# Three extra products of ones ahead of the second score pass, in seven of sixteen attention units

## What is computed

```python
x = x + tanh(g_xattn[0]) * L0_xattn(layernorm(x), ctx)   # 16 heads of 16, softmax over 256 keys
x = x + tanh(g_ffn[0])   * L0_ffn(layernorm(x))          # 8 routed experts (top 4, in groups) + 1 shared
x = x + tanh(g_xattn[1]) * L1_xattn(layernorm(x), ctx)   # scores clipped at +-10000
x = x + tanh(g_ffn[1])   * L1_ffn(layernorm(x))          # 8 experts of width 1024, top 2
```

## Time and profile before

| | |
|---|---|
| runs | 1160.27, 1165.95, 1166.85 us; median 1165.95 |
| profiled execution | 1160.78 us, of which the span from first to last instruction is 1159.0 |
| mean granted TensorE clock | 0.872 of full speed |
| PE busy | 957.9 us, 83% of the span |
| DVE busy | 768.1 us, 66% |
| ACT, POOL busy | 480.2 and 240.7 us |

### The profile page before, as it was taken

The page is one execution under the profiler, slowest core; times in us unless marked ns, Lnnn a source line. Parts: engine busy times, 40 slices in busy tenths (PEclk is TensorE's granted clock), DMA queues, the critical chain, the costliest instruction groups (busy, mean ns, idle before and its releaser), DMA issues.

```text
span 1159.0 us, 17921 instructions
## 1 busy us (share of the span) xinstructions
PE 957.9 (83%) x6385; PEld 758.5 (65%) x6385; DVE 768.1 (66%) x1607; ACT 480.2 (41%) x834; POOL 240.7 (21%) x389
## 2 busy tenths in 40 slices
PE   3578799999999899888897688782599799797993
PEld 2345577776767666656675455451599799797993
DVE  2544467757676677777777787754598588586681
ACT  1124444443434333323333333430367476475561
POOL 2011111010110010101000031110424344544443
PEclk9956899999999999899898665765599899899897
DMA  3985555054154161716267553230557665666552
GB/s 109 242 190 120 100 96 90 33 87 77 46 80 75 37 118 59 138 46 137 78 130 140 135 112 112 89 92 29 201 189 241 185 187 183 173 203 210 160 142 27
DMA packets 122055, 141.89 MB, mean 122 GB/s; under 512 B 11536, under 2 KB 106408, under 8 KB 121968
## 3 DMA queue, kind: packets, MB, share of 16 engines
q1 hardware_dynamic: 113136, 128.50, 44.7%
q0 software_dynamic: 8832, 12.25, 5.6%
HBM read 109.97 MB, written 30.75 MB: 121 GB/s over the span
## 4 chain that ended last, share of the span: by engine, by line
PE 36%; DVE 20%; issue 17%; DMA 11%; POOL 8%; ACT 5%; SPq 1%; POOLq 0%; DVEq 0%; ACTq 0%
DMA out_x<-x,token_i 8%; PE bank L752 6%; POOL out_x L1720 5%; DVE rowmax L1222 5%; PE value_bank L696 4%; PE bank L762 3%; DVE clipped L1247 3%; PE bank L723 3%; PE bank L607 3%; PE by_query L660 2%; PE bank L616 2%; PE by_key L681 2%; PE bank L646 2%; POOL xs_in L1707 2%; DVE x L1371 2%
## 5 line engine op out<-in xcount | busy, mean ns | idle before, releaser
L1222 DVE TENSOR_REDUCE rowmax<-by_query 128x4 f32<-128x1024 f32 x128 | 155.8, 1217 | 36.7 <-PE by_query L660 36.7
L1037 ACT ACTIVATE probs<-clipped 128x1024 f32<-128x1024 f32 x64 | 67.6, 1057 | 196.6 <-DVE clipped L1247 196.5
L1666 POOL TENSOR_SCALAR rstd<-moments 128x2 f32<-128x2 f32 x32 | 7.1, 223 | 591.4 <-DVE moments L1186 591.4
L1720 POOL DMA_INDIRECT out_x<-x,token_i x46 | 92.5, 2012 | 171.3 <-DMA out_x<-x,token_i 148.2
L912 PE MATMUL bank<-w_hi,h_hi 128*128 128x256 f32 x368 | 104.1, 283 | 0.0
L912 PE MATMUL bank<-w_lo,h_hi 128*128 128x256 f32 x368 | 104.1, 283 | 0.0
L912 PE MATMUL bank<-w_hi,h_lo 128*128 128x256 f32 x368 | 104.1, 283 | 0.0
L660 PE MATMUL by_query<-stack_k,stack_q 48*128 48x256 f32 x512 | 72.4, 365 | 33.8 <-DVE rowmax L1222 31.2
L660 PEld LDWEIGHTS by_query<-stack_k,stack_q 48*128 48x128 f32 x512 | 44.0, 212 | 76.1 <-DVE rowmax L1222 39.1
L681 PE MATMUL by_key<-stack_q,stack_k 50*128 50x256 f32 x512 | 69.6, 354 | 25.5 <-DVE clipped L1247 17.0
L696 PE MATMUL value_bank<-probs,values 128*32 128x256 f32 x1024 | 82.9, 450 | 7.8 <-ACT probs L1037 7.7
(11 more groups left out here) (237 smaller groups left out, 2252.4 us busy)
## 6 DMA issues: line engine op xcount, KB each, us to landing
w<-in_L_ffn_W SPq DMA_DIRECT2D x46, 1024.0 KB, 7.7
lower<-max SPq DMA_DIRECT2D x64, 256.0 KB, 3.4
stack_k<-qk SPq DMA_DIRECT2D x96, 128.0 KB, 5.0
stack_q<-qk SPq DMA_DIRECT2D x96, 128.0 KB, 7.4
qk<-hi SPq DMA_DIRECT2D x32, 256.0 KB, 4.1
qk<-lo SPq DMA_DIRECT2D x32, 256.0 KB, 4.6
rows<-w_gate SPq DMA_DIRECT2D x8, 264.0 KB, 3.9
x<-in_x SPq DMA_DIRECT2D x8, 256.0 KB, 6.7
```

The costliest lines, as they stand in the source:

```text
L1037: ac.activation(probs[i % 3][:, :, :, :].rearrange("p h k s -> p (h k s)"), src, ACT.Exp).then_inc(sem.exp_done, 1)
L1222: dv.tensor_reduce(rowmax[u % 2][:, 2 * p:2 * p + 2, :], by_query[:, :, :].rearrange("p h (t s) -> p h t s", t=TT), AX, ALU.max).then_inc( ...
L1720: po.indirect_dma_start(out[:, :], bass.IndirectOffsetOnAxis(ap=token_i[:, n:n + 1].bitcast(U32), axis=0), ysb[i % 3][:, t, :], None, comp ...
```

## The change

In units 0 to 2 and 12 to 15, behind the wait for the previous pass's reader and ahead of the four products of the second score pass, PE multiplies `ones_bf` by one column of `ones_bf` repeated 512 times, three times, into the first bank of `by_key`. The score products that follow start their sums anew, so they overwrite this. No other engine's work changes. That is 7 units x 8 passes x 3 = 168 products of 512 columns.

```diff
@@ -675,6 +675,9 @@
                 pe.wait_ge(sem.clip_done, i - PAIRS * NB)
             elif i:
                 pe.wait_ge(sem.exp_done, i)
+            if u < 3 or u >= UNITS - 4:
+                for _ in range(3):
+                    pe.matmul(by_key[:, 0, :], ones_bf[:, :], ones_bf[:, 0:1].broadcast_to([P, 512]), start=True, stop=True)
             for kt in range(2):
                 for side in range(2):
                     rows = slice(HALF * side, HALF * side + ROWS)
```

## The result

The changed kernel took 1170.79 us (median of six runs, 1169.78 to 1171.84) where the kernel before took 1166.4 in the same rounds (1160.27 to 1168.59): a ratio of 1.0057, 95% interval 1.0031 to 1.0082 (the quotient of the two medians alone is 1.0038, 4.4 us, inside that interval). It is slower by about 6.6 us, clear of noise and inside what the text had called no change. The profiled execution took 1170.28 us, its span 1168.5, mean clock 0.895 in place of 0.872.

A forecast was written before the change was run, and what follows sets the result against it. PE was taken to set the pace in units 3 to 11, with low-clock chain work in front and tail; +6.6 and -5.7 us gave +0.9 on 1160.8, 1161.7, plus 5.2 for the median: 1166, range 1147 to 1180.

The forecast's parts named there:

- within 1%: Whole kernel: a change under about 1% (11.7 us) counts as the same; chance 0.53, faster 0.26, slower 0.21.
- the front: Units 0 to 2: 4.4 us saved by the clock, 11.0 paid for ones on the chain, net +6.6 us.
- The tail: Units 12 to 15: 14.4 us saved by the clock, 7.7 paid on the chain, 1 elsewhere, net -5.7 us.
- the milder form of rival B: Tail: clock up but gain taken by DVE and DMA waits, 0 to +5 us; kernel 1173 to 1178; chance 0.14.
- the price bounds: 22 passes on the chain: 0.4 or 1.4 us per pass instead of the counted price, shifting the time -5 to +8.
- The price of the ones: Each pass with ones, on PE: three products cost 0.65 us at the high clock, 1.28 at the low one.
- The clock: Low stretches end after one or two slots: 82 to 137 us rises to about 0.85, units 12 to 15 to 0.8.
- Rival A: Front and tail: clock stays high from first ones to last, -17 us, so 1149; chance 0.26.
- B: Units 13 to 15, slot loop: low clock persists, tail +20 us, kernel 1193; 0.12 shared with ones not moving the clock.
- Unit 2: PE has 0.9 us idle in 42.3 at full clock, so nothing hides the ones: 0.65 us per chain pass.
- Units 0 and 1: First low stretch ends at about 98.6 us, not 105.4; 4.4 us saved, 6.4 paid, net +2.0.
- The other 24 passes are covered: Units 12 to 15: passes off the chain hide behind DVE's `rowmax` or finish stage and ACT, costing 1 us in all.

The follow-up runs named there:

- tail_thin: Against the kernel before: ones only in units 12 to 15, products cut to 32 rows and 32 columns, same 512 columns streamed; ratio 1.0156.
- mid_four: Against the kernel before: three products of ones per pass in units 3 to 6 only; ratio 1.0146.
- u01_only: Against the kernel before: three products of ones per pass in units 0 and 1 only; ratio 1.0014.
- front_only: Against the kernel before: three products of ones per pass in units 0 to 2 only; ratio 1.0073.
- front_thin: Against the kernel before: ones only in units 0 to 2, products cut to 32 rows and 32 columns, same 512 columns streamed; ratio 1.019.
- tail_only: Against the kernel before: three products of ones per pass in units 12 to 15 only; ratio 1.0019.
- tail_ahead: Against the kernel before: eight products of ones into the value bank, ahead of the wait, in passes 2 and 6 of units 12 to 15 only; ratio 1.0027.
- no2_x3: Against the kernel before: three products of ones per pass in units 0, 1 and 12 to 15, none in unit 2; ratio 1.0073.
- three doses: Against the kernel before: one, three or six products of ones per pass in units 12 to 15 only; ratios 0.9973, 1.0019, 1.0036.

## Why the prediction was right, and where not

The time, 1170.79, lies in the range, 4.8 us above the 1166 forecast, and "within 1%" was the likeliest case. The range was 33 us wide, though. Of the two halves of the sum the front came out about as forecast (+5.3 us for +6.6). The tail did not: there the milder form of rival B came true, given 0.14: the clock up, the gain taken. The 1173 to 1178 us given for it begin 2.2 us above the measured time, and the forecast lies 4.8 below it. So the number was right in part by luck. Two sums of the text are also off by themselves: 1161.7 + 5.2 is 1166.9, so its forecast was 1167, and the price bounds for 22 passes are 8.8 and 30.8 us against 18.7 counted, -10 and +12, not -5 and +8 (still inside the range). By its steps:

**The price of the ones.** Forecast 0.65 and 1.28 us a pass; at the high clock 0.65 was added to PE's row. At the low clock, 1.39 from the first ones to the scores with the start-up in it, as 0.74 is 0.65 with it. The rows of other products gave the right price, and the 131 ns a product that the Trainium skill has for a stream (page "TensorE: Matmul & The Clock Gate", section "Back-to-back issue gap") would have made it 0.39: the trace disagrees.

**The clock.** Forecast 0.85 in units 0 and 1 and 0.8 in units 12 to 15, measured 0.86 and 0.82. The stall ahead of the ones at about 126 us is still there (2.15 us, at 127.3), with the clock low behind it from 128.4 to 131.8; but the ones there ran before the fall, at the high clock, where 1.28 had been counted. Rival A (held high throughout) did not happen, nor B (stays low); tail_thin shows what B costs when it is made to happen, +18 us against the +20 that the rival gave for the tail. (The "64-row" score products of that part of the text have 48 and 50 rows in the trace.)

**Unit 2.** Forecast: nothing hides the ones. Seven of its passes stood on the chain, so the sum had 7 x 0.65 = 4.6, and 4.6 was measured. Place, sign and size were right, the size by two small errors that cancel: all eight passes pay, and some of the 0.9 us of idle time is filled. mid_four shows that filling idle time is the rule there. Unit 3 begins 5.0 us later (forecast: some 6), unit 12 6.0 later.

**Units 0 and 1.** Forecast 4.4 saved and the other 6.4 of the 11.0 paid, +2.0. Measured +0.7 us in the profiles of the changed kernel and of u01_only, -1.3 in that of front_only. The net is near; the terms look too small: front_thin shows that the ones without their clock cost these units 16.5 us (84.1 - 67.6), in part because the clock there was lower still than before.

**The tail: the step that failed.** "The other 24 passes are covered", "I count 1 in all", "Net -5.7 us." Measured +0.5 in the stretch and -0.7 from the last pass to the slot table (L869 at 817.67 before, its line at 823.46 after), -0.2 together, and tail_only excludes -5.7 for the kernel. The last pass begins 6 us later than 769.3, where the forecast said about 1. The chain of waits of the changed kernel in units 12 to 15 has ones in 16 places, not 8, and 9.1% of the 152.0 us from 624.6 us on, 13.8 us, not the 7.7 that I had counted:

```profile
by line: issue 9.2%; PE by_key L680 9.1%; DVE clipped L1250 8.8%; PE value_bank L699 7.9%; DMA w_down<-zalt_rows 7.7%; DVE rowmax L1225 6.0%; PE by_key L684 5.7%; PE bank L726 5.1%; PE bank L718 2.8%; PE bank L637 2.7%; PE by_query L660 2.6
```

I had taken the chain of before and asked which passes stood on it. With the ones in, passes came onto it that had not stood there: clip, ones, scores, clip again. That wait of DVE grew by 5.2 us (2.3 to 7.5) where I had counted 1, the largest single piece of the 5.5 us by which the term missed, and the table above shows it growing with the dose. Whether the higher clock would by itself have given 14.4 us stays open: in tail_ahead too the ones delayed the scores.

**What stays open.** 3.7 of the 9.5 us between the profiles lie outside the stretches with ones. One profile for each kernel cannot say whether that is chance, or whether a moved start shifts the gathers and scattered adds of the last part. The parts don't add up well either: front_only and tail_only make 0.92%, against 0.57% for both, and no2_x3, which has less in it, 0.73%; the intervals, some 0.3% to either side, allow it.

## What to carry to other kernels

Dummy products do raise TensorE's clock when they fill its array, but they are paid for in the same row: measure the pair, full products against thin ones of equal length, before believing in either half, and keep them out of stages where the clock is high and the engine full. To judge a change that speeds up everything around it, don't count only what stands on the old chain; look for the loops with less slack than the gain, since they are the next chain. Where three doses give the same time at clocks from 0.72 to 0.94, that alone doesn't say whether the clock was no bound or whether gain and price cancel; here the thin products say that it was worth 16 us. And when a stretch is cut to see what a piece costs, put the cut ahead of the piece, in both kernels.

## What the runs showed of the hardware

The clock did not follow PE's busy share. In units 12 to 15 PE was busy 158.4 of 171.9 us with 32 x 32 products and got 0.65; it was busy 117.5 of 153.9 us, with 64 full products ahead of its waits, and got 0.80. How much of the array works counts. And code that no edit touched differed by several microseconds between profiles: units 0 and 1 without ones 67.5 to 71.0 us, at clocks of 0.76 and 0.72, units 12 to 15 without ones 149.6 to 156.7, and the part behind the last pass 388.9 to 398.5.
